# A fused attention kernel: self-attention values on diagonal 32x32 tiles, keys for two batches per matmul, context parts per pair

## What is computed

```
x = x + cross_attention(layernorm(x), context, context)
x = x + self_attention(layernorm(x))
x = x + mixture_of_experts(layernorm(x))
```

```
weights = jax.nn.sigmoid(scores)
weights = weights / (jnp.sum(weights, axis=-1, keepdims=True) + EPS_RENORM)
attn = jnp.einsum('bhqk,bhkd->bhqd', weights, v)
```

## Time and profile before

| | us |
|---|---|
| median of 3 runs (1345.8 to 1345.89) | 1345.84 |
| the profiled execution | 1344.86 |
| its span | 1343.0 |
| TensorE busy | 1157.5 (86%) |
| VectorE busy | 945.0 (70%) |
| ScalarE busy | 872.4 (65%) |
| GpSimd busy | 569.7 (42%) |

### The profile page before, as it was taken

One profiled execution on the slowest core, in us unless ns is written; L12 is line 12 of the kernel. 1 busy time (PEld: TensorE's weight loads), 2 busy tenths in 40 slices (PEclk: granted clock), 3 DMA queues, 4 the chain that ended last, 5 costly groups with the idle time before them and its releaser, 6 DMA issues.

```text
span 1343.0 us, 37302 instructions
## 1 busy us (share of the span) xinstructions
PE 1157.5 (86%) x14033; PEld 936.5 (70%) x14033; DVE 945.0 (70%) x2523; ACT 872.4 (65%) x2443; POOL 569.7 (42%) x1045
## 2 busy tenths in 40 slices
PE   6898889888888898889888888988898888864797
PEld 5676777767767777777767767767777677742697
DVE  3667777777777777777777777877777777763121
ACT  3676767777777667767777777667677777632131
POOL 1244454455444444444454444444444554431121
PEclk9899999999999999999999999999999999975899
DMA  6414211111211111111111111111111111000474
GB/s 148 126 47 144 84 57 43 51 54 51 52 40 45 49 52 47 50 47 39 46 48 50 49 30 50 49 49 46 50 40 39 48 48 45 14 9 13 115 225 153
DMA packets 71904, 81.93 MB, mean 61 GB/s; under 512 B 16987, under 2 KB 50732, under 8 KB 71728
## 3 DMA queue, kind: packets, MB, share of 16 engines
q1 hardware_dynamic: 65280, 75.19, 19.3%
q0 software_dynamic: 3200, 3.71, 0.8%
q10 hardware_dynamic: 3248, 0.66, 0.2%
HBM read 64.79 MB, written 16.56 MB: 61 GB/s over the span
## 4 chain that ended last, share of the span: by engine, by line
DVE 33%; PE 31%; ACT 20%; issue 9%; POOL 6%; SPq 0%; DVEq 0%; DMA 0%; ACTq 0%; POOLq 0%
ACT prob L739 8%; ACT wbd L799 4%; PE score L444 4%; PE vps L411 4%; PE kps L401 4%; DVE prob L974 4%; ACT qz L728 3%; DVE nmx L963 3%; PE shared L477 3%; PE shared L532 3%; PE shared L523 3%; PE score L670 3%; PE score L684 3%; DVE pr L1116 3%; POOL ctx_p L1273 2%
## 5 line engine op out<-in xcount | busy, mean ns | idle before, releaser
L739 ACT ACTIVATE prob<-score,nmx 128x257 f32<-128x257 f32 x512 | 236.2, 476 | 175.8 <-DVE nmx L963 175.0
L401 PE MATMUL kps<-ctx_p,wk_p 128*128 128x256 f32 x1536 | 213.6, 289 | 0.2 <-POOL ctx_p L1273 0.2
L411 PE MATMUL vps<-wv_p,ctx_p 128*128 128x256 f32 x1536 | 212.7, 288 | 0.0
L1273 POOL TENSOR_TENSOR ctx_p<-ctxT,ctx_p 128x512 fp32r<-128x512 f32 x128 | 152.1, 1188 | 119.8 <-ACT ctx_p L755 119.8
L411 PEld LDWEIGHTS vps<-wv_p,ctx_p 128*128 128x128 f32 x1536 | 192.6, 192 | 12.4 <-issue 12.4
L401 PEld LDWEIGHTS kps<-ctx_p,wk_p 128*128 128x128 f32 x1536 | 195.4, 192 | 5.4 <-issue 2.3
L963 DVE TENSOR_REDUCE nmx<-score 128x2 f32<-128x514 f32 x256 | 163.1, 679 | 15.7 <-PE score L428 15.7
L1291 POOL TENSOR_TENSOR plast<-const,prob 128x128 f32<-128x128 f32 x128 | 64.1, 501 | 257.7 <-DVE prob L974 257.7
L974 DVE TENSOR_SCALAR prob<-prob,rsum 128x257 f32<-128x257 f32 x512 | 158.3, 352 | 9.0
L444 PE MATMUL score<-const,prob 128*128 128x128 f32 x1024 | 145.7, 280 | 7.5 <-DVE prob L974 3.5
L444 PEld LDWEIGHTS score<-const,prob 128*128 128x128 f32 x1024 | 114.1, 142 | 44.4 <-DVE prob L974 28.6
(11 more groups left out here) (163 smaller groups left out, 2188.4 us busy)
## 6 DMA issues: line engine op xcount, KB each, us to landing
ctxT<-in_ctxT SPq DMA_DIRECT2D x128, 257.0 KB, 3.0
w<-in_w SPq DMA_DIRECT2D x16, 1024.0 KB, 9.7
xq<-in_x SPq DMA_DIRECT2D x32, 128.0 KB, 3.3
xr<-in_x SPq DMA_DIRECT2D x32, 128.0 KB, 2.5
qbd<-qkT SPq DMA_DIRECT2D x256, 16.0 KB, 1.8
out<-row SPq DMA_DIRECT2D x32, 128.0 KB, 1.9
slots<-row SPq DMA_DIRECT2D x10, 257.0 KB, 5.6
x_a<-slots SPq DMA_DIRECT2D x8, 129.0 KB, 2.1
```

Of the source, the lines that this page charges most:

```text
L401: last = mm(kps[:, c, :], wk_p[:, x, n, c * P:(c + 1) * P], ctx_p[:, g, y, n, :], start=(n, x) == (0, LO), stop=(n, y) == (C - 1, LO))
L411: last = mm(vps[:, c, :], ctx_p[:, g, x, n, c * P:(c + 1) * P], wv_p[:, y, n, :], start=(n, x) == (0, LO), stop=(n, y) == (C - 1, LO))
L739: last = af(prob[:, m, :], score[:, m, 0:S], ACT.Exp, bias=nmx[:, m:m + 1], scale=1.0, accum_out=esum[:, m:m + 1])
L1273: g.tensor_tensor(ctx_p[:, g_, LO, :, :], ctxT[:, r, :, g_, 0:SM], ctx_p[:, g_, HI, :, :].bitcast(F32), ALU.subtract).then_inc(s["ctx_part ...
```

## The change

1. Self-attention values: `wbd` and the two products over it go. For each head and batch one matmul on rows and columns 32j to 32j + 31 of the array takes the 32x32 block of `th` as weights and streams `v2a`, 16 features of v and a column of ones, so that the sum comes out beside the values, with the tokens on the partitions: 64 matmuls at (1, 2). VectorE adds 2e-8, inverts 16 sums per row and multiplies (`att2n`, in quarter 1). TensorE transposes the result at (2, 1) and ScalarE copies it to `att2` in quarter 2. Place (1, 3) is empty.
2. Keys: the two batches of a pair are the 512 columns of one matmul. A quarter makes one half of the features (`c`) for the next pair, 6 matmuls, and ScalarE evacuates them in one instruction.
3. Context parts: `ctx_p` and `kT` hold both batches of a pair and have two pair slots. ScalarE's and GpSimd's parts are made for a pair, in quarters 1 and 3; in quarter 3 ScalarE's now stands ahead of `probsT` (it stood behind). GpSimd writes the last keys of a pair at once, also in quarters 1 and 3. SP's loads wait for the pair's count.

```diff
-        ctx_p = sb("ctx_p", [P, 2, 2, C, SM], F32R)
+        ctx_p = sb("ctx_p", [P, 2, 2, C, 2, SM], F32R)
-        kT = sb("kT", [P, 2, C, S])
+        kT = sb("kT", [P, 2, C, 2, S])
...
-                sp.wait_ge(s["ctx_parts"], floor0(TB * t + 2 * r - 2))
+                sp.wait_ge(s["ctx_parts"], floor0(2 * t + r - 1))
...
+            def keys(t, r, c):
+                pe.wait_ge(s["ctx_parts"], 2 * t + r + 1)
+                pe.wait_ge(s["k_evac"], 4 * t + 2 * r + c)
+                for n in range(C):
+                    for x, y in PASSES:
+                        last = mm(kps[:, :, :], wk_p[:, x, n, c * P:(c + 1) * P], ctx_p[:, r, y, n, :, :],
+                                  start=(n, x) == (0, LO), stop=(n, y) == (C - 1, LO))
...
-            def weight_sums(t):
-            def weighted_values2(t):
...
+            def self_values(t):
+                pe.wait_ge(s["sig_flat"], t + 1)
                 pe.wait_ge(s["v2_done"], t + 1)
...
+                for h in range(H):
+                    for j in range(TB):
+                        rows = slice(32 * j, 32 * j + 32)
+                        last = mm(shared[rows, h * (HD + 1):(h + 1) * (HD + 1)], th[rows, h * L:(h + 1) * L], v2a[rows, h, :],
                                   start=True, stop=True)
                 last.then_inc(s["pv2_ps"], 1)
...
-                    (1, 2): s2 and (lambda: (turn("sm_step", 2 * (t2 + 1)), weight_sums(t2))),
-                    (1, 3): s2 and (lambda: (turn("ext2_step", 2 * (t2 + 1)), weighted_values2(t2))),
+                    (1, 2): s2 and (lambda: (turn("att2n_done", t2 + 1), self_values(t2))),
+                    (2, 1): s2 and (lambda: (spare_free(xa, i, 2), transpose_rows(att2n, "att2n_done", t2, "at2_ps", spare_c))),
...
+            def keys(t, r, c):
+                act.wait_ge(s["k_done"], 4 * t + 2 * r + c + 1)
+                act.wait_ge(s["s_done"], floor0(2 * (TB * (t - 1) + 2 * r + 2)))
+                af(kT[:, r, c, :, 0:SM], kps[:, :, :], ACT.Identity, bias=b_k[:, c:c + 1], scale=1.0).then_inc(s["k_evac"], 1)
+            def context_hi(t, r):
+                act.wait_ge(ctx_in[r], 16 * C * (t + 1))
+                act.wait_ge(s["v_done"], floor0(TB * (t - 1) + 2 * r + 2))
+                af(ctx_p[:, r, HI, :, :, :], ctxT[:, r, :, :, 0:SM], ACT.Copy).then_inc(s["ctx_hi"], 1)
...
-                    v.memset(wbd[:], 0.0).then_inc(s["zeroed"], 1)
+                    v.memset(v2a[:, :, HD:HD + 1], 1.0).then_inc(s["zeroed"], 1)
...
-            def sigmoid_block(t, j):
-            def sums2(t):
-            def extract2(t):
...
+            def inverse2(t):
+                dve.wait_ge(s["pv2_ps"], t + 1)
+                v.tensor_scalar(ssum[:, :], sh_heads[:, :, HD], 2e-8, None, ALU.add).then_inc(s["ssum_step"], 1)
+                dve.wait_ge(s["ssum_step"], 2 * t + 1)
+                v.reciprocal(rsum2[:, :], ssum[:, :]).then_inc(s["ssum_step"], 1)
             def weigh2(t):
...
+                v.tensor_tensor(att2n[:, :].rearrange("p (h d) -> p h d", d=HD), sh_heads[:, :, 0:HD],
+                                rsum2[:, :].unsqueeze(2).to_broadcast([P, H, HD]), ALU.mult).then_inc(s["att2n_done"], 1)
...
+            def context_lo(t, r):
+                pool.wait_ge(s["ctx_hi"], 2 * t + r + 1)
+                g.tensor_tensor(ctx_p[:, r, LO, :, :, :], ctxT[:, r, :, :, 0:SM], ctx_p[:, r, HI, :, :, :].bitcast(F32),
                                 ALU.subtract).then_inc(s["ctx_parts"], 1)
```

More of the change, by code:

```diff
@@ L429, in scores @@
                                   qz[rows, half, e, j, :, :].rearrange("p h q -> p (h q)"),
-                                  kT[rows, b_slot(j), e, :], start=True, stop=True)
+                                  kT[rows, j // 2, e, j % 2, :], start=True, stop=True)
                         if e and m % 2:
@@ L517, in scores2 @@
                 last.then_inc(s["s2_ps"], 1)
-            def weight_sums(t):
[L520 to L526, removed]
-            def weighted_values2(t):
-                pe.wait_ge(s["v2_done"], t + 1)
[L530 to L533, removed]
+            def self_values(t):
+                pe.wait_ge(s["sig_flat"], t + 1)
+                pe.wait_ge(s["v2_done"], t + 1)
+                if once(t):
+                    pe.wait_ge(s["zeroed"], 2)
+                for h in range(H):
+                    for j in range(TB):
+                        rows = slice(32 * j, 32 * j + 32)
+                        last = mm(shared[rows, h * (HD + 1):(h + 1) * (HD + 1)], th[rows, h * L:(h + 1) * L], v2a[rows, h, :],
                                   start=True, stop=True)
@@ L572, in _ @@
             pe.wait_ge(s["wparts_done"], 2)
-            keys(0, 0)
+            for c in range(C):
+                keys(0, 0, c)
             values(0, 0)
@@ L608, in body @@
                     short(j, 0)
-                    if ahead:
-                        keys(ta, ja)
+                    if xa and (j < 2 or q):
+                        keys(i + j // 2, 1 - j // 2, j % 2)
                     short(j, 1)
@@ L790, in sigmoid_exp @@
                 af(sneg[:, :], sneg[:, :], ACT.Exp, scale=float(-SCALE)).then_inc(s["sneg_exp"], 1)
-            def sigmoid_blocks(t, batches):
-                if once(t):
-                    act.wait_ge(s["zeroed"], 2)
-                act.wait_ge(s["sig_flat"], t + 1)
-                for j in batches:
-                    b = slice(32 * j, 32 * j + 32)
-                    af(wbd[b, :, b], th[b, :].rearrange("p (h q) -> p h q", h=H), ACT.Copy).then_inc(s["sig_done"], 1)
             def gate_exp(t):
@@ L821, in _ @@
             last.then_inc(s["klast_done"], 1)
+            keys(0, 0, 0)
             context_hi(0, 1)
-            keys(0, 0)
+            keys(0, 0, 1)
             values(0, 0)
@@ L862, in body @@
                         values(ta, ja)
-                    if xa and j < 3 and (j < 2 or q):
-                        context_hi(*((i, j + 2) if j < 2 else (i + 1, j - 2)))
+                    if q and j % 2:
+                        context_hi(i + 1, j // 2)
                     if j == 0 and s2:
@@ L1363, in body @@
                 for j in range(TB):
-                    if xa and (j < TB - 1 or q):
-                        last_key(*((i, j + 1) if j < TB - 1 else (i + 1, 0)))
+                    if xa and j % 2 and (j < 2 or q):
+                        last_keys(i + j // 2, 1 - j // 2)
                     if j == 0 and once(i):
@@ L1377, in body @@
                         rms(t1)
-                    if xa and (j < 2 or q):
-                        context_lo(*((i, j + 2) if j < 2 else (i + 1, j - 2)))
+                    if q and j % 2:
+                        context_lo(i + 1, j // 2)
                     if j == 0 and s1:
```

104 lines of the change are left out of this document (27 added, 77 removed).

## The result

The changed kernel took **1364.24 us** (median; 1362.71 to 1364.74) against 1345.87 (1345.80 to 1346.71) of the kernel before in the same comparison: ratio 1.0133, 95% interval 1.0117 to 1.0149, slower by 1.3%. The forecast of 1320 was wrong, and the result lies outside its range of 1288 to 1350. The profiled execution took 1364.06 us, its span was 1362.2.

What follows compares the result with a forecast made beforehand. TensorE was taken as nearly full (32.81 of 36.74 us a step), with waits to remove. Thirty steps at -1.5 (-45.0), 29 holds (+26.7) and ends -7.6 gave -25.9, so 1320 us; range 1288 to 1350, the forecast's own 1306 to 1336.

Steps and rivals of the forecast that it cites:

- Small matmuls: TensorE's 64 self-attention matmuls in quarter 1, 128 passes: 1.8 us, ends 0.86 and 2.8.
- The pace of 12.5 ns: Time assumed per pass of the small matmuls, a little under L459's 15.5 ns: 1.6 us for 128.
- rival D: The stall only moves: small matmuls of 2.5 to 2.7 us, 1345 us; chance 0.06.
- Quarter 1: TensorE's 1.19 us stall for wbd goes and quarter 2's scores start earlier: -1.0 us a step.
- quarter 2: VectorE's qk evacuation is no longer held up by self-attention reciprocals and a product: -0.5 us a step.
- The hold: VectorE's short pr (L1116), on quarter 0's chain, waits out GpSimd's longer subtraction under a shared port lock: +0.92 us a step.
- Rival B: The hold doesn't grow, because GpSimd starts when VectorE's last operand pair is through: 1293 us; chance 0.20.
- Keys: Key matmuls, 6 of 512 columns instead of 12 of 256 per batch: same columns stream, counted 0.
- Start and end: First key groups +1.4 us, wbd memset gone -2.1, last step's self-attention -5.2, step before it -1.7: together -7.6.
- Rival C: Small matmuls bound by a fixed price each, TensorE stretches quarter 1: 1398 us; chance of passing its deciding point 0.18.
- floor of about 25 ns from start to start: Skill's issue gap for 1 to 64 columns: 128 passes take 3.2 us, estimate 1362; counted in C's chance.

Runs made afterwards that it cites:

- e17: e1 run again unaltered (kernel before with the self-attention part of the change alone): 1282.23 us, ratio 0.9530.
- e2: The kernel before with the paired keys and paired context parts alone, wbd kept: 1379.98 us, ratio 1.0250.
- e10: The kernel before with the self-attention part and the early context copy, keys and context per batch: 1254.84 us, ratio 0.9330.
- e13: The changed kernel run again unaltered: 1336.80 us, ratio 0.9936.
- e14: The changed kernel with the second pair's high-part copy moved to the end of quarter 2, run again unaltered: 1270.55 us (first 1305.75), ratio 0.9444.
- e18: e10 run again unaltered: 1254.66 us, ratio 0.9321.
- e1: The kernel before with the self-attention part of the change alone, keys and context per batch: 1338.66 us, ratio 0.9941.
- e6: The kernel before with ScalarE's high-part copy of the next tile's second batch moved from quarter 3 to the end of quarter 2: 1314.72 us, ratio 0.9772.
- e8: The changed kernel with the 64 small matmuls spread among quarter 1's 12 value matmuls, five after each: 1568.15 us, ratio 1.1657.

## Why the prediction was wrong, point by point

**The parts add up where the pauses are short.** The span of e17 is 62.5 us under that of before, the span of e2 35.4 over it (it holds four falls): together -27.1, which is 1317.8 for the profiled execution; the forecast's sum was -25.9, 1319.0. What the change then took, 1336.8, is 19 us more, for 18 falls at about 1.1 us. The result's span is 27 more again: 0.67 us in each undisturbed step (36.63 against 35.96), so 20 us, and five more falls. Against the forecast's 1319.0 the result's 1364.06 is 45 us too long: some 25 for 23 falls, some 20 for the pauses.

- **Small matmuls, 1.8 us with ends 0.86 and 2.8: the term of the sum that failed in the result.** They took 2.6. In e10, e13, e14, e17 and e18 the same block took 1.75. The pace of 12.5 ns was an average over something that isn't even: in the row of 45, passes go out 8.6 ns apart ((0.56 - 0.18) / 44; the 7.2 of some expectations is near the median distance, 7 to 8 ns), and pauses come between. The forecast kept 2.6 within its ends, and put "no gain" at 2.7; rival D gave it 1345. The lower end of the forecast's own range, 1306, doesn't follow from its terms: 0.86 us was -1.3 a step, which is 1311.
- **Quarter 1, -1.0, and quarter 2, -0.5: a little too small.** e17 gained 1.78 us a step (36.74 to 34.96), with the block at 1.75.
- **The clock: the step that failed, not in the sum at all.** All terms were priced at clock 1.00 because the trace of before shows that. The change puts a block with pauses ahead of the probability transposes, and it lengthens TensorE's waits around quarter 0: 0.60 us for att and a new 0.54 for probT, beside the unchanged 1.14. The wait for att was 0.33 us in the kernel before; order of time:

```profile
640.13 0.17 PE L550 MATMUL gather<-oh,tri_bf 128*128 128x8 bf16 x1 [0.33 <-DVE att L985]
```

Each fall costs 1.1 us (37.74 - 36.63), twice what a step was to gain (36.75 - 36.2). No bound of the forecast covered this: it takes 19 of the 27 us that the parts give (e13), and with the long pauses the sign turns.
- **The hold, +0.92: right.** pr went from 1077 to 1903 ns, e2's step by +0.87. The Trainium skill's rule ("SBUF — State Buffer", "SBUF: two separate sides") that the lock lasts as long as GpSimd's instruction agrees: 2.09 beside 2.17 us. Rival B is excluded.
- **Keys, 0: right.** 208.2 / 768 = 271 ns against twice 139.
- **Start and end, -7.6: the sum about right (8 us gained in all outside the 28 steps, against 9.7), its parts not.** Outside the 28 steps e17 gained 15 us where the sum had 12.0 (-2.1, -5.2, -1.7, and two more steps at -1.5), and e2 lost 7 where it had 2.3 (1.4 and one more hold).
- **Rival C** had the right sign by another mechanism: not a fixed price of each load. The Trainium skill's floor of about 25 ns from start to start ("TensorE: Matmul & The Clock Gate", "Back-to-back issue gap"), which gave 1362, is close to the result by accident: no run here shows it, with 8.6 ns apiece in a burst and 2.6 / 128 = 20 ns with the longest pauses.

What stays open is what makes the pauses long or short. The kernel is excluded (e13, e14, e17). The loading of instructions isn't seen in them either: in e1, 7 of the 28 blocks have no instruction packet of 16 KB (queue 8) that starts between 2 us ahead of them and 2.5 us behind their start, and their pauses add up to 1.20 us (median) as in the other 21. The pauses were long in the result and in the first group, short in the four other groups, each on another chip; whether it is the chip or where the program lies in its memory wasn't told apart. Why quarter 0's same waits bring a fall in 18 steps of e13 and in 4 of e2 wasn't tested either. That taking the waits away takes the falls away is shown (18 in e13, 1 in e14).

## What to carry to other kernels

Look for what an instruction of another engine holds before merging it into a longer one: here one early copy (e6) was worth more than the whole change, and with the self-attention part it gave 6.7%, or 8.2% with weights and values rounded to bfloat16. Price a block of very short matmuls with its pauses, by a range, and run it on more than one chip before believing a result of 1%. When a change puts idle time or tiny instructions on an engine that ran at the full clock, add a rival in which the clock falls, at some 1 us each time here.

## What the runs showed of the hardware

- The same kernel, unaltered, took 1364.24 and 1336.80, 1305.75 and 1270.55, 1338.66 and 1282.23 us in different groups, while the medians of the kernel before, which has no block of short matmuls, stayed within 1344.9 and 1346.1.
- A value matmul and ten small passes behind it took 0.53 us a round (e8), 0.3 more than the two by themselves: some 0.15 us for each change between the whole array and 32x32 tiles, if that is the cause.
- In e8 the granted clock stayed at 1.2 GHz for 10.2 us in each of the 28 steps while TensorE showed as busy throughout: an engine that the profile shows as busy can be at half its clock.
